# Attention layer in float32 on one core: the softmax sums and their inverses move in one transfer for both heads instead of two

## The reference

```python
q, k, v = x @ w_q, x @ w_k, x @ w_v               # 16 heads of 64
logits = q @ k.T / sqrt(64); masked where key > query
out = softmax(logits) @ v @ w_o
x = layernorm(x + out)
h = butterfly(gelu(butterfly(x @ W_exp + b_exp) + up_bias))
x = layernorm(x + h @ W_con + b_con + down_bias)
```

## Time and profile before

| | us |
|---|---|
| median of 3 runs | 1208.28 (1206.38 to 1210.69) |
| the profiled execution | 1209.85 |
| its span on the chip | 1207.8 |
| PE busy | 1124.5 |
| DVE, ACT, POOL busy | 728.8, 650.3, 758.4 |

### The profile page before, as it was taken

One profiled execution on the slowest core, in us unless ns is written; L12 is line 12 of the kernel. 1 busy time (PEld: TensorE's weight loads), 2 busy tenths in 40 slices (PEclk: granted clock), 3 DMA queues, 4 the chain that ended last, 5 costly groups with the idle time before them and its releaser, 6 DMA issues.

```text
span 1207.8 us, 18944 instructions
## 1 busy us (share of the span) xinstructions
PE 1124.5 (93%) x5880; PEld 725.1 (60%) x5880; DVE 728.8 (60%) x2029; ACT 650.3 (54%) x1294; POOL 758.4 (63%) x722
## 2 busy tenths in 40 slices
PE   5899999999899999999899999999899999998897
PEld 4566555665666656565765555665765556653666
DVE  5766666665666666664566666665466666650555
ACT  3466666663466666663366666664366566643231
POOL 6377777776377767676177777777176676667102
PEclk9899999999999999999999999999999999998999
DMA  6122222221222222221222221221122222110002
GB/s 197 36 68 67 54 71 71 54 72 37 61 54 66 69 54 71 72 53 36 61 63 54 71 71 48 68 62 38 45 63 71 53 48 51 47 36 18 10 9 61
DMA packets 63633, 69.83 MB, mean 58 GB/s; under 512 B 26759, under 2 KB 35243, under 8 KB 63534
## 3 DMA queue, kind: packets, MB, share of 16 engines
q1 hardware_dynamic: 63534, 68.64, 21.9%
HBM read 32.15 MB, written 2.36 MB: 29 GB/s over the span
## 4 chain that ended last, share of the span: by engine, by line
PE 69%; DMA 9%; issue 6%; DVE 6%; ACT 3%; SPq 3%; POOL 3%; DVEq 0%; POOLq 0%; ACTq 0%
PE O L683 14%; PE WORK L634 12%; PE SC L666 9%; PE SC L662 9%; PE WORK L722 5%; DMA QL<-NROW 4%; PE WORK L651 4%; PE WORK L614 3%; PE WORK L616 3%; PE WORK L622 3%; PE WORK L615 3%; PE WORK L778 3%; DMA R<-RROW 2%; DMA RROW<-RCOL 2%; SPq L394 2%
## 5 line engine op out<-in xcount | busy, mean ns | idle before, releaser
L867 ACT ACTIVATE PR<-SC 128x512 f32<-128x512 f32 (+3 forms) x768 | 351.4, 490 | 273.4 <-PE SC L666 254.5
L515 POOL TENSOR_TENSOR SUM<-SUM,PR 128x1024 f32<-128x1024 f32 (+3 forms) x256 | 416.9, 1628 | 10.1
L683 PE MATMUL O<-PR,VP 128*64 128x512 f32 (+3 forms) x1536 | 293.0, 500 | 3.7 <-POOL PR L500 3.7
L666 PE MATMUL SC<-QL,KH 128*128 128x512 f32 (+3 forms) x768 | 265.1, 351 | 19.6 <-DMA QL<-NROW 19.6
L662 PE MATMUL SC<-QH,KHL 128*128 128x512 f32 (+3 forms) x768 | 268.4, 355 | 5.4 <-ACT PR L867 4.3
L500 POOL TENSOR_SCALAR_AFFINE_SELECT PR<-PR 128x256 f32<-128x256 f32 x256 | 107.0, 418 | 262.4 <-ACT PR L867 261.9
L989 DVE CUSTOM_DVE_ANT_0 WORK<-WORK,CMASK 128x128 f32<-128x128 f32 (+3 forms) x512 | 240.2, 510 | 34.2 <-PE WORK L634 34.0
L634 PE MATMUL WORK<-KHL,QH 128*128 128x512 f32 (+3 forms) x768 | 233.5, 377 | 11.5 <-DVE MP L989 6.4
L992 DVE TENSOR_REDUCE MP<-WORK 128x1 f32<-128x512 f32 x256 | 165.0, 686 | 84.1 <-PE WORK L634 84.1
L634 PEld LDWEIGHTS WORK<-KHL,QH 128*128 128x128 f32 x768 | 136.2, 190 | 97.1 <-issue 54.4
L662 PEld LDWEIGHTS SC<-QH,KHL 128*128 128x128 f32 x768 | 145.5, 189 | 81.2 <-ACT PR L867 41.2
(11 more groups left out here) (95 smaller groups left out, 1052.7 us busy)
## 6 DMA issues: line engine op xcount, KB each, us to landing
QH<-QH SPq DMA_DIRECT2D x128, 128.0 KB, 2.3
KH<-KHL SPq DMA_DIRECT2D x128, 128.0 KB, 2.3
R<-RROW SPq DMA_DIRECT2D x128, 128.0 KB, 2.8
SW<-in_L_ffn_up_weights_dram SPq DMA_DIRECT2D x9, 512.0 KB, 4.6
SW<-_L_ffn_down_weights_dram SPq DMA_DIRECT2D x9, 512.0 KB, 4.8
RCOL<-R SPq DMA_DIRECT2D x128, 2.0 KB, 1.8
out_dram<-X SPq DMA_DIRECT2D x8, 256.0 KB, 2.3
QL<-NROW SPq DMA_DIRECT2D x64, 4.0 KB
```

The lines of the kernel that those rows point to most:

```text
L515: nc.gpsimd.tensor_tensor(total, total, prob(unit, s), ALU.add).then_inc(add_done, 1)
L666: nc.tensor.matmul(dst, KH1[:, par, h, kt * P:(kt + 1) * P], QL[:, par, h, q0:q0 + n], start=False, stop=True).then_inc(scores_ready, 1)
L683: t = nc.tensor.matmul(O[qc][h * K:(h + 1) * K, START[s]:], VP[:, par, kt, h * K:(h + 1) * K], p[:, h, :], start=kt == 0, stop=s == LAST_O ...
L867: nc.scalar.activation(prob(unit, s)[:, h, :], SC[use % NSC][:, 0:n], ACT.Exp, scale=K ** -0.5).then_inc(exp_done, 1)
```

## The change

Both pairs of transfers become one transfer each. The fold reads the two partitions 0 and 64 of R0 in one access, as 2 rows of 64 pieces of 8 values, into the 128 partitions of RCOL. The broadcast reads RROW as 2 rows, each repeated 64 times, into the 128 partitions of R. The semaphores count 16 for each pair instead of 32. Nothing moves in the order of any engine.

```diff
                 sp.wait_ge(sums_out, (norms + 1).value())
-                for h in range(2):
-                    sp.dma_start(RCOL[h * K:(h + 1) * K, 0, :], R0[h * K:h * K + 1, :].rearrange("a (p e) -> a p e", p=K))\
-                        .then_inc(sums_landed, 16)
+                sp.dma_start(RCOL[:, 0, :], R0[0:P:K, :].rearrange("a (p e) -> a p e", p=K)).then_inc(sums_landed, 16)
                 sp.wait_ge(recip_made, (norms + 1).value())
                 sp.wait_ge(o_free, (norms + O_CREDIT).value())
                 sp.dma_start(RROW.rearrange("h (p e) -> (h p) e", p=K), RCOL[:, 1, :]).then_inc(recip_landed, 16)
                 sp.wait_ge(recip_landed, (norms.times(16) + 16).value())
-                for h in range(2):
-                    sp.dma_start(R[h * K:(h + 1) * K, :], RROW[h:h + 1, :].broadcast_to([K, CH])).then_inc(inverse_landed, 16)
+                sp.dma_start(R[:, :], RROW.rearrange("(h a) n -> h a n", a=1).broadcast_to([2, K, CH])).then_inc(inverse_landed, 16)
...
-            sp.sem_inc(sums_landed, 32)
+            sp.sem_inc(sums_landed, 16)
...
-                    act.wait_ge(sums_landed, (norms.times(32) + 32).value())
+                    act.wait_ge(sums_landed, (norms.times(16) + 16).value())
...
-                dve.wait_ge(sums_landed, (norms.times(32) + 64).value())
+                dve.wait_ge(sums_landed, (norms.times(16) + 32).value())
...
-                dve.wait_ge(inverse_landed, (norms.times(32) + 32).value())
+                dve.wait_ge(inverse_landed, (norms.times(16) + 16).value())
```

## The result

The changed kernel takes 1548.3 us (median of 4 runs, 1546.1 to 1551.5) against 1208.3 before (4 runs): a ratio of 1.2815, interval 1.2778 to 1.2851. It is 340 us slower. The prediction was 1485, range 1340 to 1610.

What follows compares the result with a forecast made beforehand. The prediction took PE, busy 93% of the span, as the bound. Its terms, 105 + 92 - 6 + 9 + 77 = 277 us on 1209.85, gave 1487, put at 1485 for the median; range 1340 to 1610.

Steps and rivals of the forecast that it cites:

- Two engines: Each merged transfer, with outermost source count 2, gets two DMA engines, 64 of the 128 rows on each.
- The rival with 16 engines: The merged broadcast keeps 16 engines, data for the scale of qc 1 ending up to 0.55 us earlier: 1195 us; chance 0.11.
- The broadcast: Broadcast of the inverses: 64 packets per engine at 0.089 us take 5.7 us, so the scale starts 3.9 us later.
- Term 1: In windows, PE stalls behind the late scale of qc 1, which has no slack: 27 x 3.9 = 105 us.
- Term 2: PE waits 3.3 us longer for `QL<-NROW`, queued behind the broadcast of qc 0, 28 times: 92 us, less 6.
- The rival of the free rows: `QL<-NROW` uses other engines or passes the two-engine broadcast, so PE's longer wait and its clock loss go: 1360 us; chance 0.05.
- Term 3: In the four flushes the scale waits longer for its broadcast: 4 x 2.3 = 9 us.
- Term 4: The merged fold lands when it did before, with one issue of about 0.57 us gone: cost taken as 0.
- Term 5: SP has two issues fewer per chunk, 0.55 us each, but waits for NROW or rows are stuck: 0.
- Term 6: PE's clock falls after nearly every new stall: 1.4 us x 55 = 77 us, bounds 0 and 88.

Runs made afterwards that it cites:

- copies8: Against the kernel before: each head's inverses written eight times to DRAM, one merged broadcast reading 16 rows, each repeated 8 times; 1289 us, ratio 1.0644.
- bcast_qc0: Against the kernel before: one broadcast for both heads for chunk 0 only, two for chunk 1; 1383.1 us, ratio 1.1434.
- fold_only: Against the kernel before: only the fold is one transfer, the broadcast stays two; 1209.5 us, ratio 0.9996.

## Why the prediction was right

**Two engines.** Right. The packets show 2 small ones per merged transfer, and the series of 64, 8 and 4 could be read on to 2. The rival with 16 engines is refuted for this change, and its mechanism seen in `copies8`: one transfer instead of two is the better one there, where the merged access keeps 16 engines.

**The broadcast.** 5.7 us of data were predicted and some 6.0 came; issue to scale 7.25 and 7.5. DVE's waits for the broadcast were to be near 110 + 64 x 3.9 = 360 us, and are 360.6. The prediction's lower bound for a packet on a busy engine, 0.081 us, did not follow from the 246 GB/s that it names beside it. In the plateau of the slow broadcast two engines move 49 GB/s, which is 0.084 us for a packet of 2 KB.

**Term 1.** 105 us predicted, 100.7 measured in PE's list of waits.

**Term 2.** The mechanism was right, the size wasn't. 92 - 6 = 86 us were predicted, 119.2 came. The term put PE's start 0.45 us after the broadcast's last packet. In the window shown it is 9.0 us behind the broadcast's issue (648.15), 1.7 more than the 7.35 of the working. The trace splits this. The first two held rows pass at 655.5, where the working had the broadcast's end at 655.05: 0.45 us. The two of the second transfer pass at 656.35, another 0.85 later, where the working had all four pass at no cost. And PE starts at 657.19, 0.84 behind them instead of 0.45. The window is one of the worst: over the 28 the start is 7.7 to 9.4 us behind the issue, and the waits are 5.2 us on average in the 16 windows with a load of weights behind the rows, and 4.7 in the other 12. What the load has to do with it is not shown. `bcast_qc0` confirms that this stall is this broadcast's doing alone. The rival of the free rows is refuted for SP's queue: 4 of 16 rows wait.

**Term 3.** 9 us predicted, 7.2 measured.

**Term 4, the fold.** 0 predicted, and `fold_only` shows 0.9996.

**Term 5.** 0; not tested by itself, but `fold_only` has one issue fewer for each chunk and gains nothing.

**Term 6, the clock.** The step with the largest miss: 77 us predicted, 112 measured as the rise of PE's busy time, or 2.0 instead of 1.4 us for each of 55 stalls. The working took the loss from a flush, where PE had stood 2.4 us and lost 1.6, and set the bounds at 0 and 88; the 112 lie outside them. But the stalls here are 3.5 to 5.8 us, half clock lasted 3.0 to 6.4 us behind them, and half of that time is lost. The one loss after a short stall was taken as the most that a long one could cost. Together, 35 us of term 6 and 33 of term 2 are the 63 us between 1485 and 1548, less the few of the other terms. That 1548 still lies in the range is partly luck: the 125 us of room upward were worked out for a transfer of 7.8 us, the transfer took 6.0, and the room was used up by a longer way from the broadcast to PE's start and by the clock.

The signs for each rival that the prediction named were the right ones to look at: small packets, GB/s, and PE's wait for the rows. PE's busy share was to be under 80% and came to 79.9% (1236.7 of 1548.3).

## What to carry to other kernels

Before two transfers are merged, look at the outermost count of both accesses: with 64 and 16 a transfer had 16 engines here, with 8, 4 and 2 that many, with 62 two. The small packets in the DMA view tell how many engines a transfer had. And when PE bounds the kernel and gets stalls of several microseconds, add the clock's loss behind them, here half of the stalls' own length (112 us for 227).

## What was not expected of the hardware

- Half clock after a stall of PE of 3.5 to 5.8 us came every time and lasted 3.0 to 6.4 us: 2.0 us of loss per stall over 55 stalls.
- One broadcast of 256 KB on 16 engines moves in 1.1 us at up to 397 GB/s (`copies8`), the same bytes in two transfers issued 0.55 us apart in 1.8.
- A small transfer in another queue passes a large one only in part: PE's wait for the rows fell from 139 to 110 us. And behind a load of 512 KB issued 0.3 us earlier and beside copies issued in the same microsecond, 4 KB took 5.3 us from issue to use instead of 2.6.
